# Routing arithmetic of a mixture-of-experts layer, issued in one block or spread over ten hidden blocks

## The reference

```python
shared = _swiglu(flat @ w_in.T) @ w_out.T
g_probs = softmax(flat @ wg.T + gb)              # 2 groups
g_idx = argmax(g_probs)
e_logits = flat @ we.T + eb                      # 8 experts, 4 in a group
masked = where(g_idx[:, None] == egid[None, :], e_logits, -inf)
p_expert = softmax(masked) * g_prob              # g_prob: probability of the chosen group
topv, topi = top_k(p_expert, 2)
w_se = zeros(S, 8).at[arange(S)[:, None], topi].add(topv)
h = _swiglu(flat @ w1.T)                         # silu(a) * b, hidden size 2048
routed = sum over e of (h * w_se[:, e:e+1]) @ w2[e].T
out = x + shared + routed
```

## Time and profile before

| | us |
|---|---|
| median of 3 runs | 4669.14 (4663.87 to 4671.28) |
| the profiled execution | 4682.31 |
| its span, slowest core (core 6) | 4681.2 |
| its other cores | 4644.2 to 4666.6 |
| TensorE busy | 3839.1 (82%) |
| VectorE busy | 1132.4 (24%) |
| ScalarE busy | 483.6 (10%) |
| granted TensorE clock, mean | 0.908 on core 6, 0.910 to 0.911 on the others |

### The profile page before, as it was taken

How to read it: one execution, slowest core, us unless ns; L and a number is a source line. 1 busy time by engine, 2 the same in 40 slices (tenths; PEclk the granted TensorE clock), 3 DMA queues, 4 the chain that set the end, 5 groups by cost and what they waited for, 6 DMA issues and landing times.

```text
span 4681.2 us, 46346 instructions; the slowest of 8 cores (4644.2 to 4681.2 us)
## 1 busy us (share of the span) xinstructions
PE 3839.1 (82%) x17629; PEld 1715.0 (37%) x17976; DVE 1132.4 (24%) x2213; ACT 483.6 (10%) x753; POOL 119.4 (3%) x226
## 2 busy tenths in 40 slices
PE   4558623149995789999979999979999996999999
PEld 1213201014442334444434444434444443444444
DVE  0150311014454311222321122241112223111111
ACT  1110110014442101000010100001000000110000
POOL 0000000000000000000000000000000000000000
PEclk8769866579997899999989999989999997999999
DMA  5440599982212213222221322222132213112111
GB/s 90 73 125 0 67 119 116 120 118 55 64 55 89 65 63 111 80 101 104 87 76 37 131 81 81 86 108 72 36 117 105 98 50 117 54 59 113 72 72 72
DMA packets 71321, 391.16 MB, mean 84 GB/s; under 512 B 10160, under 2 KB 10160, under 8 KB 59328
## 3 DMA queue, kind: packets, MB, share of 16 engines
q0 software_dynamic: 23328, 237.11, 22.1%
q1 hardware_dynamic: 36864, 100.68, 7.1%
q10 hardware_dynamic: 10912, 50.40, 3.0%
HBM read 423.81 MB, written 88.08 MB: 109 GB/s over the span
## 4 chain that ended last, share of the span: by engine, by line
PE 76%; DMA 7%; another core or an unknown queue 7%; DVE 6%; issue 2%; DVEq 1%; ACT 1%; POOL 0%; ACTq 0%; POOLq 0%; SPq 0%
PE ps_r L1134 19%; PE ps_tb L1134 19%; PE ps_a L1060 4%; PE ps_tb L1060 4%; PE ps_r L1067 4%; PE ps_b L1067 4%; PE ps_r L1099 3%; PE ps_kv L355 2%; PE ps_tb L1099 2%; PE ps_id L355 2%; DMA w<-w2s 2%; PE ps_id L511 2%; PE ps_q L355 2%; DMA xf<-x 1%
## 5 line engine op out<-in xcount | busy, mean ns | idle before, releaser
L1134 PE MATMUL ps_r<-w,hsT 128*128 128x512 bf16 x4012 | 908.2, 382 | 41.0 <-DMA w<-w2s 36.5
L1134 PE MATMUL ps_tb<-w,hsT 128*128 128x512 bf16 x4016 | 900.1, 379 | 4.2
L1134 PEld LDWEIGHTS ps_r<-w,hsT 128*128 128x128 bf16 x4096 | 402.5, 98 | 527.7 <-issue 50.6
L1134 PEld LDWEIGHTS ps_tb<-w,hsT 128*128 128x128 bf16 x4096 | 400.8, 98 | 483.3
L355 PE MATMUL ps_kv<-wtk_b,xT_b 128*128 128x512 bf16 x497 | 132.2, 420 | 311.3 <-ACT xT_b L352 310.1
L1060 PE MATMUL ps_a<-hiT,wab 128*128 128x512 bf16 x1004 | 245.7, 398 | 129.5 <-DMA wab<-wabs 117.5
L1142 DVE SCALAR_TENSOR_TENSOR acc<-ps_tb,wse,acc 128x1024 f32<-128x1024 f32 x128 | 164.3, 1284 | 720.1 <-PE ps_tb L1134 720.1
L1142 DVE SCALAR_TENSOR_TENSOR acc<-ps_r,wse,acc 128x1024 f32<-128x1024 f32 x128 | 164.3, 1284 | 672.0 <-PE ps_r L1134 672.0
L1060 PE MATMUL ps_tb<-hiT,wab 128*128 128x512 bf16 x1004 | 229.7, 379 | 1.6 <-DMA wab<-wabs 0.3
L1067 PE MATMUL ps_b<-hiT,wab 128*128 128x512 bf16 x1004 | 229.7, 379 | 1.1
L1067 PE MATMUL ps_r<-hiT,wab 128*128 128x512 bf16 x1000 | 229.5, 379 | 1.3
(11 more groups left out here) (202 smaller groups left out, 2643.8 us busy)
## 6 DMA issues: line engine op xcount, KB each, us to landing
w<-w2s POOLq DMA_DIRECT2D x64, 2048.0 KB, 13.1
w2s<-w2T POOLq DMA_DIRECT2D x8, 4096.0 KB, 378.5
wab<-wabs POOLq DMA_DIRECT2D x128, 256.0 KB, 3.0
wab<-wabs SPq DMA_DIRECT2D x128, 256.0 KB, 2.7
xf<-xp SPq DMA_DIRECT2D x32, 512.0 KB, 3.7
xf<-x SPq DMA_DIRECT2D x32, 512.0 KB, 4.8
x1s<-x_sb SPq DMA_DIRECT2D x32, 512.0 KB, 5.7
x1t<-x1s SPq DMA_DIRECT2D x32, 512.0 KB, 9.3
```

Source lines behind the costliest of these rows:

```text
L1134: mi = PE.matmul(pr[:, 512 * h:512 * (h + 1)], hsT[:, hc * CH + i * 128: hc * CH + (i + 1) * 128], w2_b[bi][:, hc * D + 512 * h: hc * D + ...
```

## The change

The routing arithmetic of step 4 is no longer issued ahead of the hidden blocks. It is issued inside the `hc` loop of kind 0, behind each block's `hsT` product: `s1_gate_a` of tile `hc`, `s1_gate_b` of tile `hc - 1` and `s1_gate` of tile `hc - 2`. The semaphores that passed once for all 8 tiles now pass for each tile. The arithmetic itself is the same.

```diff
@@ s1_gate_a(i)
-                    if i == TPC - 1:
-                        DVE.engine_nop().then_inc(sv_g, 1)
-                        ctr["g"] += 1
+                    DVE.engine_nop().then_inc(sv_g, 1)
+                    ctr["g"] += 1
+                    ga_cnt[i] = ctr["g"]
@@ s1_gate_b(i)
-                    if i == 0:
-                        ACT.wait_ge(sv_g, ctr["g"])
-                        if c > 0:
-                            ACT.wait_ge(sv_se, c * TPC)
+                    ACT.wait_ge(sv_g, ga_cnt[i])
+                    if i == 0 and c > 0:
+                        ACT.wait_ge(sv_se, c * TPC)
...
-                    if i == TPC - 1:
-                        ACT.nop().then_inc(sc_gx, 2)
-                        ctr["gx"] += 2
+                    ACT.nop().then_inc(sc_gx, 2)
+                    ctr["gx"] += 2
+                    gb_cnt[i] = ctr["gx"]
@@ s1_gate(i)
-                    if i == 0:
-                        DVE.wait_ge(sc_gx, ctr["gx"])
+                    DVE.wait_ge(sc_gx, gb_cnt[i])
@@ chunk loop, ahead of the kinds
-                for i2 in range(TPC):
-                    s1_gate_a(i2)
-                for i2 in range(TPC):
-                    s1_gate_b(i2)
-                for i2 in range(TPC):
-                    s1_gate(i2)
-                gx_done[c] = ctr["gx"]
@@ hc loop, behind the hsT product
                         DVE.engine_nop().then_inc(sv_sT, 1)
+                        if kind == 0:
+                            if hc < TPC:
+                                s1_gate_a(hc)
+                            if 1 <= hc <= TPC:
+                                s1_gate_b(hc - 1)
+                            if 2 <= hc <= TPC + 1:
+                                s1_gate(hc - 2)
+                            if hc == TPC + 1:
+                                gx_done[c] = ctr["gx"]
```

More of the change, by code:

```diff
@@ L827, in build_nc @@
             gx_done = {}
+            ga_cnt = {}
+            gb_cnt = {}
             gx_ln = {}
```

## The result

| | before | changed |
|---|---|---|
| median, undisturbed runs | 4669.14 us (5 runs) | 4555.64 us (7 runs) |
| ratio, 95% interval | | 0.9752 (0.9731 to 0.9773) |
| profiled execution | 4682.31 us | 4551.48 us |
| mean span of the 8 cores in it | 4660.0 us | 4537.7 us |

The forecast was 4551.4 us, range 4539 to 4582; 4669.14 x 0.9752 is 4553.3 us. In part of the executions the cores of a die show a lower granted clock and take longer (up to 5320 us), and the times and ratios here leave these out.

What follows compares the result with a forecast made beforehand. The prediction took TensorE (82% busy) to bound the kernel, stalled by a late-issued weight load. Gain 124.4 us, less 6.0 for handoffs and 0.7 for transfers, took 4669.1 to 4551.4 us, range 4539 to 4582.

Steps and rivals of the forecast that it cites:

- What the stall was: TensorE ahead of block 2: waits 29 us a chunk for a weight load issued late behind routing arithmetic and `hsT`.
- Gross gain: TensorE around block 2: four waits, 117.5 us, and slow first groups after them, 6.9 us, both go: 124.4 us.
- The sum: Whole kernel: 124.4 - 6.0 - 0.7 = 117.7 us off the median 4669.1, giving 4551.4 us; chance 0.84.
- the handoff: Block's matmuls through silu's table load to next weights: 7.21 us against 6.90, five of nine pay, 6.0 us in all.
- the `acc` load: Chunks 1 to 3: the 4 MB load meets block 2's weight load, costing 0.7 us, between 0 and 2.1.
- VectorE costs nothing: VectorE in kind 0: product and passes take 5.7 us of a 6.90 us block, leaving 1.2 us free.
- The lag of the passes: VectorE's new waits: `s1_gate(hc-2)` needs exponentials run behind the silu of block hc-1, so they do not hold it.
- The first rival: ScalarE's table switches cost more than their load, 25.6 to 28 us on paying handoffs: 4577 to 4579 us, chance 0.10.
- The second rival: TensorE's waits for `w2` blocks grow, giving back up to 29 us a chunk: 4660 to 4669 us, chance 0.03.
- The third rival: VectorE needs over 6.90 us between products, delaying blocks 2 to 9; 4708 us at 12 us a block, chance 0.02.

Runs made afterwards that it cites:

- block_behind_1: Kernel before, with the whole routing arithmetic as one block behind the product of hidden block 1: 4690.8 us; on another chip, ratio 1.0047 to the kernel before.
- gate_twice: Changed kernel with VectorE's routing arithmetic executed twice for each tile: 4619.9 us, ratio 0.9925 to the kernel before.
- no_lag: Changed kernel with all three passes of a tile behind the product of the same block: ratio 0.979 to the kernel before.
- no_switch: Changed kernel with a tile's two exponentials replaced by Identity, so no table load stands between silus in the blocks: ratio 0.9746 to the kernel before.
- dear_switch: Changed kernel with an added tiny silu and exponential, with drains, ahead of silus of blocks 0 and 2 to 9: 4611.9 us, 0.9896 of the kernel before.
- shared_stage_2: Changed kernel with routing arithmetic behind the additions of the shared output instead of kind 0's products, second run: 4535.9 us, 0.9733 of the kernel before.
- shared_acc_late: shared_stage_2 with the 4 MB load of acc issued behind the silu of block 4 instead of at the chunk's start: 4557.1 us, 0.9781 of the kernel before.

## Where the prediction held, and the step that failed

- **What the stall was.** Right: routing arithmetic, then `hsT`, then the weight load. The wait went when VectorE was no longer held in one piece, and block_behind_1 shows that the piece counts, not which product is late.
- **Gross gain.** 124.4 us forecast, 126.0 measured: 118.2 for the waits, 7.0 for the cold groups (the excess of blocks 2 to 15 before), and 0.8 at block 0, which was not expected and is within what that start varies by (34.3 to 37.1 us on the slowest cores of all runs). Less the 0.4 and 3.1 that the changed kernel pays, that is 122.5.
- **The sum.** The forecast of 4551.4 us lies 4.2 us from the measured 4555.6, closer than its terms deserve, and that is luck. Of the two costs one was put too high and the other too low (the handoff and the `acc` load, below), 6.7 us forecast and 5.5 measured by the mean of the cores; and the gain in time, 114 us here and 123 us on another chip, varies by more than either.
- **VectorE costs nothing.** Right, with the forecast margin: 1.2 us said, 1.28 us seen. gate_twice and no_lag both cross it and cost somewhat more than worked out (82 for 74, 35 for 29).
- **The lag of the passes.** The prediction said that VectorE's new waits do not hold it; no_lag shows that this is the lag's doing, worth 35 us of kind 0.
- **The handoff.** This is the step that failed, and its path was right: the price of the table loads was put at 5 x 0.3 x 4 = 6.0 us and measured 3.1, half of it (3.3 by the mean of the cores), one part in 40 of the gain. The fault is in "Add 1.29 for the table, the transfer, and 0.25 to TensorE's start", whose transfer, 2.83 us, was the mean of the four that ended a stall; these spread from 2.45 to 3.26 us, more than the shortfall of 0.3 us that was drawn from them. One handoff of the changed kernel, all engines:

```profile
1549.70 3.62 PE L1053 MATMUL ps_tb<-hiT,wab 128*128 128x512 bf16 x15
...
1553.82 0.32 SPq L1039 DMA_DIRECT2D wab<-wabs  x1
...
1556.74 1.46 PE L1053 MATMUL ps_a<-hiT,wab 128*128 128x512 bf16 x6
```

  Block start to load issue is 4.12 us (4.13 forecast), but from issue to matmul it is 2.92 us, not 3.08. The handoff is 7.04 us and short by 0.14, not by 0.3. Blocks 3 to 15 of the four chunks have 16 starts that are late by more than 0.05 us, where 20 were forecast with those of block 2: 15 by 0.07 to 0.29 us, and block 11 of chunk 2 by 0.9 us. That last one is late by 0.7 to 1.1 us on all eight cores and on time in no_switch; on core 0 its weight load took 3.44 us, and why just this one is slow was not found. That each pair of handoffs pays once, five times in a chunk, is shown by dear_switch, where the price is large enough to see.
- **The first rival, a dearer switch.** Excluded by no_switch, dear_switch and the timeline. Its figure, a drain of about 1380 ns with each switch, is the Trainium skill's ("ScalarE: Activation LUTs", "What ACT_TABLE_LOAD costs"); here 0.19 us lie between the end of one function and the load, 0.01 us between load and the other function. The page's 1283 ns for the load itself agrees with the mean of the changed kernel's 68 loads. Its advice to group activations by table set holds in direction, but was worth only some 3 us here. What cost 122 us was not the grouping but where the block stood: shared_stage_2 groups the exponentials too (12 loads) and has no stall.
- **The second rival, gain given back.** Excluded: the waits for `w2` blocks are 50.6 us against 55.7, and the cores' mean span fell by 122.3 us where the stage gave 121.1.
- **The third rival, slower.** Its mechanism is real, though not in this change: VectorE's 5.7 us a block cost nothing, 7.9 us (no_lag) cost 35 us, and 10.4 us (gate_twice) took two thirds of the gain. That the loss begins at the period, 6.9 us, fits these three points; nothing between 5.7 and 7.9 was run.
- **The `acc` load.** Also mis-sized, the other way: 0.7 us forecast, in chunk 1 and hardly in 2 and 3. Core 0 has the 0.4 us of the table, but the mean of the eight cores is 2.2 us and the highest 3.7, above the bound of 2.1; and chunk 3 has the most, up to 1.8 us on one core. The step at fault is "hardly in 2 and 3, which are alike". shared_acc_late shows that about two thirds of this lateness in chunks 1 to 3 come from the load; what the rest comes from is open.

## What to carry to other kernels

A block of small operations on an engine that is busy 25% of the time can hold the busiest engine for its whole length when a buffer's release stands behind it in the queue; spread it so that each piece, with the work already there, fits into one period of the busiest engine. Give a pass that needs another engine's answer to the last one a lag of a period, or its wait is paid in every piece. A table load ahead of an activation is paid after the wait, but with two buffers only by every second handoff, and only by what it exceeds the slack. Where another stage has no release waiting behind the block, the block can stand there whole, with fewer table loads.

## What the runs showed of the hardware that was not expected

- One 4 MB load in flight took a 256 KB load from 2.7 to 9.24 us. Issued at the chunk's start, it costs block 2 one or two us in all; issued behind the silu of block 4, it costs 21 us.
- Waits of about the same length had different sequels. In dear_switch the next group of matmuls took 3.61 us after 3.07 us (chunk 0) and 6.47 us after 3.12 us (chunk 2); in gate_twice it took 5.30 us after 3.18 us (block 5 of chunk 0, granted clock 0.66) and 3.62 us after 3.55 us (chunk 1, granted clock 1.00). After 4.90 us, in shared_acc_late, it took 5.30 us:

```profile
1562.00:1567.00 5.00, 5.00 (x16) 1.97 (x17) 0.00 (x0) 0.00 (x0) 0.00 (x0) 0.66 1.03 405
```
